# Three cross attentions of a four-layer decoder: score maxima from stacked operands, scores computed again in turned form instead of transposed probabilities

## What is computed

```python
q = (x @ Wq + bq)   # 16 heads of 16 columns
k = (ctx @ Wk + bk); v = (ctx @ Wv + bv)
attn = einsum('bhqd,bhkd->bhqk', q, k) * 0.25
# layer 0 clips attn to +-10000, layer 1 puts the most negative number where the mask is false
attn = softmax(attn, axis=-1)
y = einsum('bhqk,bhkd->bqhd', attn, v).reshape(B, N, 256)
# layers 0 and 1: y @ Wo + bo;  layer 3: relu(y @ W1 + b1) @ W2 + b2
```

## Time and profile before

| | |
|---|---|
| median of 3 runs | 1796.17 us (1795.55 to 1798.46) |
| span of the profiled execution | 1785.6 us |
| between the span and the median | 10.6 us |
| PE busy | 1579.5 us (88% of the span), 14786 instructions |
| DVE busy | 941.3 us (53%) |
| ACT busy | 717.5 us (40%) |
| POOL busy | 409.0 us (23%) |
| mean granted clock of PE | 0.957 |
| part 1, first key product to last residual | 151.1 to 341.4 us |
| part 4, the same | 654.3 to 834.7 us |
| part 10, the same | 1345.5 to 1543.6 us |

### The profile page before, as it was taken

How to read it: one execution, slowest core, us unless ns; L and a number is a source line. 1 busy time by engine, 2 the same in 40 slices (tenths; PEclk the granted TensorE clock), 3 DMA queues, 4 the chain that set the end, 5 groups by cost and what they waited for, 6 DMA issues and landing times.

```text
span 1785.6 us, 40853 instructions
## 1 busy us (share of the span) xinstructions
PE 1579.5 (88%) x14786; PEld 1305.9 (73%) x14786; DVE 941.3 (53%) x2546; ACT 717.5 (40%) x1675; POOL 409.0 (23%) x627
## 2 busy tenths in 40 slices
PE   7998998799987879998797788997988999899998
PEld 6876776678975657776687566775876777689897
DVE  3665877511116657777110562556345667565864
ACT  3334876232323336652222314551755556211110
POOL 2224776500004421112000233432121111000101
PEclk9998999999998999998899798998998999999999
DMA  5343000278951011102686001001001000033232
GB/s 212 147 151 121 28 27 19 106 279 300 321 185 35 1 53 44 29 15 87 254 290 228 13 1 58 28 27 48 1 1 66 23 26 15 24 96 117 81 108 68
DMA packets 41852, 166.72 MB, mean 93 GB/s; under 512 B 5985, under 2 KB 16865, under 8 KB 30177
## 3 DMA queue, kind: packets, MB, share of 16 engines
q1 hardware_dynamic: 39392, 159.14, 25.7%
q0 software_dynamic: 2304, 5.51, 1.0%
HBM read 140.21 MB, written 24.41 MB: 92 GB/s over the span
## 4 chain that ended last, share of the span: by engine, by line
PE 70%; DVE 12%; issue 7%; DMA 3%; POOL 3%; ACT 3%; SPq 1%; DVEq 0%; POOLq 0%; ACTq 0%
PE bank L1688 7%; PE bank L1701 6%; PE bank L1268 6%; PE bank L1630 4%; PE bank L1255 4%; PE bank L1631 4%; PE bank L1632 4%; PE bank L1282 3%; PE bank L795 2%; PE bank L804 2%; PE bank L1238 2%; PE bank L1243 2%; PE bank L896 1%; PE bank L782 1%; DMA xrow<-slots 1%
## 5 line engine op out<-in xcount | busy, mean ns | idle before, releaser
L2053 ACT ACTIVATE arena<-big,nm 112x375 f32<-112x375 f32 x384 | 215.9, 605 | 29.5 <-DVE nm L2894 16.4
L1268 PEld LDWEIGHTS bank<-cst,arena 112*125 112x125 f32 x1152 | 146.6, 192 | 54.0 <-issue 29.0
L1268 PE MATMUL bank<-cst,arena 112*125 112x112 f32 x1152 | 168.0, 283 | 8.8 <-ACT big L2063 5.0
L3150 POOL TENSOR_TENSOR mv<-mv,cst 112x1 f32<-112x1 f32 x88 | 20.1, 228 | 607.3 <-DVE mv L2283 607.3
L2202 ACT ACTIVATE htile<-bank,wup 128x128 f32<-128x128 f32 x280 | 79.7, 368 | 189.7 <-PE bank L1688 189.6
L1688 PE MATMUL bank<-xtile,wup 128*128 128x128 f32 x1120 | 132.8, 278 | 0.3 <-DVE xtile L2997 0.2
L1688 PEld LDWEIGHTS bank<-xtile,wup 128*128 128x128 f32 x1120 | 129.8, 194 | 1.0 <-DVE xtile L2997 0.9
L3013 DVE COPY yrow<-bank 128x256 f32<-128x256 f32 x35 | 14.8, 424 | 217.5 <-PE bank L1701 217.5
L1701 PE MATMUL bank<-wdn,htile 128*128 128x256 f32 x560 | 126.3, 379 | 0.0
L2897 DVE TENSOR_SCALAR_CACHE_REDUCE big<-bank 112x375 f32<-112x375 f32 x192 | 96.0, 543 | 35.3 <-PE bank L1255 33.6
L1701 PEld LDWEIGHTS bank<-wdn,htile 128*128 128x128 f32 x560 | 103.9, 190 | 12.8
(11 more groups left out here) (359 smaller groups left out, 3571.7 us busy)
## 6 DMA issues: line engine op xcount, KB each, us to landing
wup<-in_moe_up SPq DMA_DIRECT2D x35, 1028.0 KB, 7.3
wdn<-in_moe_dn SPq DMA_DIRECT2D x35, 1024.0 KB, 6.1
vspace<-in_ring SPq DMA_DIRECT2D x40, 512.0 KB, 4.2
ctxs<-parts SPq DMA_DIRECT2D x30, 564.0 KB, 3.9
slots<-mlpw SPq DMA_DIRECT2D x11, 1024.0 KB, 6.5
parts<-ctxs SPq DMA_DIRECT2D x8, 564.0 KB, 3.1
xrow<-slots SPq DMA_DIRECT2D x35, 128.0 KB, 5.0
slots<-yrow SPq DMA_DIRECT2D x35, 128.0 KB, 7.0
```

The costliest lines, as they stand in the source:

```text
L1268: mm = pe.transpose(bank[4 + (3 * g + t) % 2][0:KT, j * T:(j + 1) * T], c_pr[:, g, j, t * KT:(t + 1) * KT], ident[0:T, 0:T])
L2053: nc.scalar.activation(c_pr[:, g, j, :], c_sc[:, g % 2, j, :], ACT.Exp, bias=nm[:, p, h:h + 1], scale=-1.0).then_inc(cexp_done, 1)
```

## The change

A group of four heads is now computed from stacked operands. The queries and keys are split into a rounded high part and the rest; three blocks of 32 rows stand on top of each other, for the queries high, low, high and for the keys high, high, low, so that one fp32r product over 96 rows gives the sum of the three partial products.

- `k_high` and `k_low` (ACT and DVE, one pair per key half) and `q_high` and `q_low` (ACT and POOL) make the parts in `k_hl` and `q_hl`. SP copies them to the stacks with 12 transfers for the keys (96 KB each) and 12 for the queries (57 KB each) per batch, `stack_keys` and `stack_queries`. There are two stacks, by parity of the batch.
- `scores` makes two products of 112 by 376 per half group into the two banks of `pair`; DVE takes the maxima of both with one reduction (`maxima`) and copies nothing out. The second half waits for the maxima of the first, the next group for those of the second.
- `shifts` (DVE, two small instructions, three in part 1) puts the negated maxima, split as well, into columns 97 to 104 of `x_nm`; `shifts_t` transposes that on PE, `joined` multiplies rows 96 to 104 with a 0/1 pattern into the query stack, beside rows of ones in the key stack.
- `scores_t` makes the scores again, keys on the rows, with the shift in the product: three tiles, two products of 125 by 224 each, into banks 4 and 5. ACT's exponential writes the tile that `values` reads. No transposes of probabilities and no copies are left.
- In part 1 POOL limits tiles 0 and 1 and DVE tile 2 (`clip`, `clipped`), to 1 and exp(-60); the maximum is clamped by one of the small instructions. In part 4 the mask is a row of the stack.
- The values of a group stand two steps behind its scores, in the step after its first tiles: behind the second turned tile of the next group and in front of its third.
- The output copy moves from DVE to ACT; keys, values and queries of the next batches are made earlier. At the start of a part POOL fills nine rows of each key stack with ones (3008 columns) and in part 4 a row of each query stack (1792 columns) ahead of it.

Elsewhere only semaphores are merged and buffers renamed.

The diff, cut:

```diff
@@ SP @@
+            def stack_keys(sub, b, p):
+                sp.wait_ge(ckl_done, at(sub, "k2", b, 2))
...
+                sp.wait_ge(ct_ready, at(sub, "c12", b - 2, 12))
...
+                for i in range(4):
+                    for r, part in enumerate((0, 0, 1)):
+                        sp.dma_start(k_st[32 * r:32 * r + 32, p, :, :].rearrange("r (m i) n -> r i m n", i=4)[:, i, :, :].bitcast(F32),
+                                     k_hl[32 * i:32 * i + 32, part, :, :].bitcast(F32)).then_inc(kst_in, 16)
...
@@ PE @@
-                    for j in range(4):
-                        pe.wait_ge(cmax_ready, at(sub, "c16", b, 4 * g + j - 3))
...
-                        pe.matmul(bank[j][0:T, 0:S2], c_qm[rows, p, g // 2, g % 2, :], c_kT[rows, p, g // 2, :],
-                                  start=True, stop=True).then_inc(cs_ready, 1)
+                def scores(b, g, p, half):
...
+                    pe.wait_ge(cmax_ready, at(sub, "p8", b, 2 * g + half))
+                    for e in range(2):
+                        mm = pe.matmul(bank[e][0:T, 0:S2P], q_st[0:rows, p, 2 * g + half, e * T:(e + 1) * T],
+                                       k_st[0:rows, p, 2 * g + half, :], start=True, stop=True)
+                    mm.then_inc(cs_ready, 1)
...
+                def scores_t(b, g, p, t):
...
+                    pe.wait_ge(cexp_done, at(sub, "c12", b, n - 1))
+                    for k in range(2):
+                        mm = pe.matmul(bank[4 + n % 2][0:KT, 2 * T * k:2 * T * (k + 1)], k_st[0:SHIFTS, p, 2 * g + k, t * KT:(t + 1) * KT],
+                                       q_st[0:SHIFTS, p, 2 * g + k, :], start=True, stop=True)
+                    mm.then_inc(ct_ready, 1)
...
-                    for j in range(4):
-                        mm = pe.transpose(bank[4 + (3 * g + t) % 2][0:KT, j * T:(j + 1) * T],
-                                          c_pr[:, g, j, t * KT:(t + 1) * KT], ident[0:T, 0:T])
...
+                    if back[1]:
+                        scores_t(*back[1], 0)
+                        scores_t(*back[1], 1)
...
+                    if back[2]:
+                        values(*back[2])
+                    if back[1]:
+                        scores_t(*back[1], 2)
@@ ACT @@
-                        nc.scalar.activation(c_pr[:, g, j, :], c_sc[:, g % 2, j, :], ACT.Exp, bias=nm[:, p, h:h + 1],
-                                             scale=-1.0).then_inc(cexp_done, 1)
+                    nc.scalar.activation(x_pt[:, g % 2, t, :], bank[4 + n % 2][0:KT, 0:4 * T], ACT.Exp).then_inc(cexp_done, 1)
@@ DVE @@
+                def maxima(b, g, half):
+                    dve.wait_ge(cs_ready, at(sub, "p8", b, 2 * g + half + 1))
+                    dve.tensor_reduce(nm[:, g % 2, 2 * half:2 * half + 2], pair[0:T, :, 0:S2], AX_X, ALU.max, negate=True)\
+                        .then_inc(cmax_ready, 1)
...
+                def joined(b, g, p):
+                    dve.wait_ge(cx_ready, at(sub, "g4", b, g + 1))
+                    out = q_st[96:SHIFTS, p, 2 * g:2 * g + 2, :].rearrange("r c (e n) -> r (c e) n", e=2)
+                    dve.tensor_tensor(out, bank[2][96:SHIFTS, 0:T].unsqueeze(1).to_broadcast([SHIFTS - 96, 4, T]),
+                                      c("join")[96:SHIFTS, :].unsqueeze(2).to_broadcast([SHIFTS - 96, 4, T]), ALU.mult).then_inc(cj_done, 1)
@@ POOL @@
                 def clip(b, g, p):
...
-                    for j in range(2, 4):
-                        h = 4 * g + j
-                        ins = nc.gpsimd.tensor_scalar(c_pr[:, g, j, :], c_pr[:, g, j, :], c_lo[:, p, h:h + 1], 1.0, ALU.max, ALU.min)
+                    for t in range(2):
+                        pool.wait_ge(cexp_done, at(sub, "c12", b, 3 * g + t + 1))
...
+                        nc.gpsimd.tensor_scalar(x_pt[:, g % 2, t, :], x_pt[:, g % 2, t, :], 1.0, math.exp(-FLOOR), ALU.min, ALU.max)\
```

More of the change, by code:

```diff
@@ L1359, in step @@
-                        if two and sub.mlp:
+                            if not one:
+                                pe.wait_ge(ckl_done, at(sub, "k2", b, 2))
+                            elif sub.mlp:
+                                pe.wait_ge(cq_done, at(sub, "c1", b + 1, 1))
+                            else:
+                                pe.wait_ge(cv_done, at(sub, "c3", b, 3))
+                            keys(b + 1, 1 - p, 0, bank[3])
+                    if g == 1 and more:
+                        pe.wait_ge(ckl_done, at(sub, "k2", b + 1, 1))
+                        keys(b + 1, 1 - p, 1, bank[3])
@@ L1364, in step @@
                             project_out(b - 2)
                     if g == 1:
[L1366 to L1371 removed]
+                        if sub.mlp and two:
+                            idle(b, 2)
+                            project_out(b - 2)
@@ new lines, in step @@
+                        if after and not sub.mlp:
+                            if two:
+                                y_taken(b - 2)
+                            q_in(b + 2, TL)
+                    if g == 2:
+                        if one:
+                            idle(b, 2)
+                            if sub.mlp:
+                                if two:
+                                    y_taken(b - 2)
+                            elif after:
+                                pe.wait_ge(cq_done, at(sub, "c1", b + 2, 1))
@@ L1418, in step @@
+                            output_rows(sub, b - 1)
+                        if more and sub.mlp:
+                            pe.wait_ge(cv_done, at(sub, "c3", b + 1, 1))
+                            value_rows(b + 1, 1 - p, 1, bank[3])
+                        if two and not one and not sub.mlp:
+                            idle(b, 5)
                             rows_t(sub, b - 2, p)
                     if g == 3:
-                        if back[0] and sub.mlp:
-                            pe.wait_ge(cv_done, at(sub, "c3", b, 1))
-                            value_rows(b, p, 1, TL)
@@ L1432, in step @@
-                        if back[0] and sub.mlp:
-                            pe.wait_ge(cv_done, at(sub, "c3", b, 2))
-                            value_rows(b, p, 2, TL)
-                        if back[2]:
-                            transposes(*back[2], 2)
-                        if (one or two) and back[0]:
-                            pe.wait_ge(cv_done, at(sub, "c3", b, 3))
+                            idle(b, 1)
+                            output_columns(sub, b - 1)
+                        if more and not sub.mlp:
+                            pe.wait_ge(cv_done, at(sub, "c3", b + 1, 2))
+                            value_rows(b + 1, 1 - p, 2, bank[3])
@@ L1449, in step @@
-                        if back[3] and not sub.mlp:
-                            values(*back[3])
-                        if one and not sub.mlp:
-                            idle(b, 1)
-                            output_columns(sub, b - 1)
+                        if after and sub.mlp:
+                            pe.wait_ge(cv_done, at(sub, "c3", b + 1, 3))
+                            q_in(b + 2, bank[3])
+                    if back[2]:
+                        values(*back[2])
+                    if back[1]:
+                        scores_t(*back[1], 2)
@@ L2923, in step @@
-                    if back[0]:
-                        scores_in(b, g, p, (0, 1))
+                    after = more and (not isinstance(b, int) or b + 2 < B)
+                    y_at = 2 if sub.mlp else 1
+                    if back[0]:
+                        maxima(b, g, 0)
+                    if back[1]:
+                        joined(*back[1])
+                    if back[2] and sub.clip:
+                        clipped(*back[2])
                     if two and g == 0 and sub.mlp:
                         output_columns(sub, b - 2)
-                    if two and g == y_at + 2:
+                    if two and g == y_at:
+                        residual(sub, b - 2, p)
@@ L2937, in step @@
-                    if back[2]:
-                        tile(*back[2], 2)
-                    if one and g == 3 and sub.mlp:
-                        output_normed(sub, b - 1)
-                    if two and g == y_at + 1:
-                        stats(sub, b - 2, p, 0)
-                    if g == 3 and more and sub.mask:
-                        row_of(b + 1, 1 - p)
+                        maxima(b, g, 1)
+                        shifts(b, g, p)
+                    if g < 2 and more:
+                        k_low(b + 1, 1 - p, g, bank[3])
```

687 lines of the change are left out of this document (370 added, 317 removed).

## The result

Median of 4 runs 1973.62 us (1972.17 to 1984.51), against 1795.86 us for the kernel before on the same chip: ratio 1.101 (95% interval 1.098 to 1.105), slower by 178 us where 6 us less was forecast. The profiled execution's span is 1971.7 us against 1785.6, the mean granted clock 0.897 against 0.957.

What follows compares the result with a forecast made beforehand. PE's instruction list was taken to bound the steady batches. Steady gain -24.6, starts +36 and +3, first three batches 0, ends -20.3 sum to -5.9 us: 1790 us against 1796.2; range 1765 to 1816 (the forecast's own 1780 to 1802).

Steps and rivals of the forecast that it cites:

- 0.43 us a transfer: SP's issue time assumed for each stack transfer; at the starts 24 transfers end their issue at 3.4 + 10.3 us.
- rival 1: SP's list binds parts 1 and 4 above 0.45 us a transfer: 1807 us at 0.48, 1835 at 0.55; chance 0.28.
- The steady stacks: SP's issue and landing of the next batch's stacks: 18.3 us in part 1, 19.2 with a mask; hidden, nothing to spare.
- First three batches: Batches 0 to 2 of each part: 166 us together against 165.6 before, so 0 change.
- Starts: First key product to first scores: +11.3, +14.7, +9.9 us, +36 for stacking operands, and +3 for the clock.
- The ring: PE and DVE waiting on each other each step: 17.5 us a batch, with additions 19.0 in part 4, 20.9 in 10.
- What goes and what comes: PE's instructions removed and added per step: 1.46 instead of 2.12 us, 0.66 less, 63 over 96 steps.
- Values in the hole: In PE's step, values (0.71 us) stand in and beyond a 0.8 us wait of the third tile for an exponential.
- POOL in part 1: POOL's limits, 1.84 us each for 448 columns, set part 1's period at 19.1 us, with POOL over 95% busy.
- Ends: Last group's scores to last residual: 18.0, 15.5 and 18.8 us, 52.3 against 72.6, so -20.3.
- Rival 4: Clock drops in steady batches as PE waits more: mean 0.9 costs 1 us in 24 batches, 1814 us; chance 0.05.

Runs made afterwards that it cites:

- mask_first: On the changed kernel, SP issues the mask's load ahead of the twelve query pieces instead of behind them: 1941.5 us, ratio 1.082.
- groups: On the changed kernel with mask_first and side-by-side stack chunks, each head group's first scores wait only for its own pieces, with reordered starts: 1873.2 us, 1.044.
- groups2: groups, with query pieces waiting for the same group's third tile two batches back, and start order keys 0-1, queries 0-1, keys 2-3, queries 2-3: 1850.5 us, 1.029.
- best2: root_last plus the edit of two_lists, plus other weight loads issued behind the last stacks in parts 1 and 4 only: 1833.9 us, 1.024.
- groups_late: groups, with the value products behind the third turned tile instead of ahead of it: 1875.5 us, 1.046.
- clip_pool: groups2, with the third tile's limit in part 1 moved from VectorE to POOL: 1851.2 us, 1.034.
- root_last: clip_pool, with the layer norm's root in part 1 last in POOL's second step, behind that step's limits instead of ahead: 1843.0 us, 1.028.
- two_lists: groups2, with batch 0's twelve query pieces of each part issued by ScalarE beside SP's twelve key pieces: 1860.4 us, 1.034.

## Why the prediction was wrong

- **The term that failed: 0.43 us a transfer.** It measured 0.64, whatever the bytes. No row of before shows that price: the four transfers of the earlier trace rows go from DRAM to SBUF, and their mean of 0.65 holds one long issue of 1.26 beside a median of 0.43, just as I read it. That 0.65 comes so near to 0.64 is chance. What failed is to take the median of another kind of transfer for copies between two places of SBUF. The text said that SP's list decides above 0.45, and rival 1 had the mechanism; at 0.64 its slope of 28 us per 0.07 gives 1871, and its sum worked out again, with part 10 in it, about 1890. The chance of 0.28 and the range up to 0.5 us rested on a price between 0.33 and 0.65 that no row supports. The rule of the Trainium skill, "DMA: Bandwidth & Descriptors", section Bandwidth, on transfers under 64 KB speaks of the transfer, not of its issue. The price here is the issue, the same for pieces of 56 and of 94 KB; whether the small ones are dominated by descriptors no run here shows.
- **The circle through the mask was missed.** "The steady stacks" counted the mask as 0.9 us more of issues. I had listed that VectorE has the mask's two passes, but not asked what the load behind them waits for, nor who stands behind them: 5.7 us a batch in the steady part of part 4, 32 us in all (mask_first). With rival 1's sum that makes some 1920 of the 1974 us. Of the rest 23 are the ends (below); what remains is not told apart.
- **First three batches, "0": +79.** Of these, 28 are batch 0 (23.5, 32.5 and 23.3 us, 17 each forecast) and 51 batches 1 and 2, which follow the same two circles as all later ones. In batch 0 of parts 1 and 10 SP starts 5.0 us behind the first scores and issues for 16.9 and 16.6 us, where 3.9 and 10.7 stood in the sum; in part 4 it pauses for the mask's reduction as well. groups and what follows it start batch 0 earlier and meet another wait: the split keys have one buffer, and ScalarE may not write batch 1's before all key pieces of batch 0 have landed (15.5 us of waiting in part 1 of groups, 10.4 in groups2, none in best2). Batch 0 lasts 24 to 31 us in these two, and 20.4 and 19.8 in parts 1 and 4 of best2.
- **Starts, +39: right in kind, 12 us short.** Forecast 17.1, 20.5 and 17.1 with the microsecond of clock in each, measured 20.5, 24.7 and 22.0. Of the difference 24 x 0.21 = 5 us is the price of a piece in each, against 0.8 us less of landing (2.0 instead of 2.8).
- **The ring, 19.0 and 20.9: right as a number, and by luck.** groups2 shows 19.35 and 21.6 once the stacks are out of the way. But the ring is not what holds it there. In part 4 the third tile stands 4.5 to 4.6 us behind its step's first pair, not 3.45, PE waits for no exponential in batches 3 to 5, and all its waits make 0.9 us a batch: as far as the profile shows, PE's own list sets the step. "What goes and what comes" had put that list at 0.66 us a step below the one before, 17.6 us a batch; 19.35 less the waits is 18.5. "Values in the hole" belongs here: the hole of 0.8 us isn't there (groups_late). In the kernel after, all this is hidden under the circles and earned nothing.
- **POOL in part 1: wrong.** A limit of 448 columns by two constants takes 0.56 us (median of 64), not 1.84, and POOL is busy for 36% of batches 3 to 5, not over 95%: the form with limits read from a tile costs 1.54 for 375 columns, and says nothing of the other. The Trainium skill, "GPSIMD Engine Reference", section 3.1, would put it at 0.67 at best, an estimate from its 1.8 cycles; the trace is still below. What holds part 1 in clip_pool is VectorE held up by POOL (root_last), which no term had; with it gone a batch takes 20.4 us, still 1.3 above the 19.1 forecast. In the kernel after the same shows in VectorE's own limits, of up to 1.72 us, but no run takes that away alone.
- **Ends, -20: not there.** 25.8, 23.5 and 26.4 us to the start of the last residual, not 18.0, 15.5 and 18.8. The clock is 0.67 to 0.81 where it was 0.93 to 1.00, PE having waited more there, and in part 4 the last values wait for an exponential that stands behind the routing's:
```profile
969.50 1.35 PE L1374 MATMUL bank<-x_pt,vspace 125*32 125x112 f32 x24 [3.11 <-ACT x_pt L2141]
```
  No run tests how the 23 us divide among these; that stays open.
- **Rival 4, the clock.** It did fall, to 0.78 in part 4's steady batches, but as a follower of the waits: it is 0.90 without the mask's (mask_first) and 1.00 without SP's (groups2). What the low clock adds to the time of the kernel after is not told apart.

## What to carry to other kernels

Price a list of small transfers by the spacing of issues in a row of the trace, of transfers between the same kinds of memory, and when the list comes near the period, follow the circle: which wait starts the list, what else is queued in it, and which engine's list stands behind that load. A load that an engine waits for, with other work behind it in its list, belongs ahead of a dozen issues, not behind them. A better steady loop must be weighed against the start that it needs: here 9 us were won in the middle batches of three parts and 51 lost at their beginnings.

## What was not expected of the hardware

- A copy between two places of SBUF costs SP 0.59 to 0.60 us of issue, with 16 or 32 partitions, 28 to 188 KB, one run or two a partition. From SBUF to DRAM it was 0.32 (k_dram), from DRAM 0.30 to 0.60. No run here shows a reason for the difference. ScalarE's list issues at nearly the same price, 0.61, beside SP's, which stays at 0.59 (two_lists).
- VectorE's normalisation took 3.19 us beside an unbroken row of POOL's, its limit of a tile (median 0.39 us) up to 1.72, and both count as busy, not idle. The Trainium skill, "SBUF — State Buffer", section "Who interferes with whom", says that the pair of ports which the two share is held by whoever starts first for its whole instruction. The trace agrees that one blocks the other, but the wait lasted over six of POOL's operations, not one.
